# Placing the negated maxima of all groups in the query stack by small matmuls instead of by a transfer

## The chip, the cores and the metric

The kernel runs on one core of one Trainium2 chip. The metric is the device time in microseconds (us) of one execution; a kernel's time is the median of its runs. Five engines work side by side on the core: TensorE (PE), VectorE (DVE), ScalarE (ACT), GpSimd (POOL) and SyncE (SP, which only issues transfers here).

## The reference, cut to what matters

Three blocks stand one after the other: cross attention over a context of 4096 keys, a chunked retention, and a mixture of eight experts. The change lies in the first:

```python
q = split_heads(layernorm(x) @ w_q.T + b_q)        # x: (2, 256, 256), 16 heads of 16
k = split_heads(ctx @ w_k.T + b_k)                 # ctx: (2, 4096, 256)
v = split_heads(ctx @ w_v.T + b_v)
scores = einsum('bhqd,bhkd->bhqk', q, k) / 4
scores = where(mask, -inf, scores)                 # mask (1, 1, 256, 4096): True is hidden
attn = einsum('bhqk,bhkd->bhqd', softmax(scores), v)
x = x + attn @ w_o.T + b_o
x = x + retention(layernorm(x), ...)
x = x + experts(layernorm(x), ...)
```

With these inputs the mask hides all keys but the last ones, and the kernel takes a fast path over one window of 896 keys (7 blocks of 128).

## The kernel before, in words

Two batches of 16 heads are worked in eight **stages**: stage `st` is batch `st // 4` and the group of four heads `st % 4`. A stage has seven **steps**, one for each block of 128 keys (`KB = 7`), so there are 56 steps, `n = 0` to 55. Queries and keys stand cut into bf16 parts in two stacks, `qstack` and `kstack`; 96 rows of a stack carry the products of the parts, and rows 96 to 99 (`MROW` to `KROWS`) carry corrections. In `qstack` these four rows hold, for each head and query, the negated maximum of its scores, cut into bf16 parts. So one matmul yields scores less the maximum, and ScalarE needs only an exp.

The work of a step, in the order in which it is written:

- **TensorE**: scores of two heads (L847, 8 matmuls in four column groups), one or two maximum tiles of the *next* stage (L772, 8 matmuls each), scores of the two other heads, then the weighted values of the step before (L865). At the second step of a stage the output of the last stage is turned (L827).
- **ScalarE**: two exps (L1325), each over 128x512; now and then a copy of outputs (L1313), keys or values.
- **VectorE**: one reduction per maximum tile (L1647); after the eighth of a stage, four small operations cut the result into parts (L1666 to L1669, tile `mpart`).

There are two score banks, so the scores of step `n + 1` wait until the exps of step `n` have read theirs. Two pairs of banks carry the maximum tiles, so a tile waits for the reduction of the tile two before it.

**How the maxima come into the stack** differs by stage. `ROWS_AT` gives the step at which it happens: `n = 4` for stage 1, then 11, 18, 25, 32, 39 and 46 for stages 2 to 7, which is three steps ahead of the stage's own first step.

- Stage 0: before the steps begin (L808, L1471 and L1473); not touched.
- Stage 1: `second_rows`, eight transposes (L819) of 4 columns each, which land in rows 96 to 99 of the last bank, then one ScalarE copy of 4x1024 right into `qstack` (L1338).
- Stages 2 to 7: `turn_rows`, two transposes (L794) of 16 columns each, a ScalarE copy of 16x256 to `mrows` (L1297, `rows_out`), and a transfer from `mrows` to `qstack`, issued by SP (L422, `load_rows`). The first scores of the stage wait for the transfer by `rows_loaded`.

All engines run their instructions in the written order. SP issues the transfers of stages 2 to 4 between its loads of keys and late weights, and those of stages 5 to 7 behind the load of the experts' weights. A second path for other masks, which loops over windows, keeps its own way in both kernels and does not run here.

Of the kernel before, what the change touches and what calls it, by code (L numbers as in the profile page):

```python
# [16 lines left out]
P = 128  # L17
NB = 2
NQ = 256
# [10 lines left out]
G = 4  # L30
NG = NH // G
STAGES = NB * NG
# [17 lines left out]
MROW = NPROD * DK  # L50
COLS = 32
KROWS = MROW + 4
# [46 lines left out]
ROWS_AT = {LAST_TILE[st] + (2 if st > 1 else 1): st for st in range(1, STAGES)}  # L99
# [61 lines left out]
class Chunk:  # L161
# [24 lines left out]

    def rows_loaded(self, st):

        n = st // 2 + 1 - (not self.loop)
        return self.at(f"mrows_loaded{st % 2}", 16 * n) if n else self.at("mrows_ready", st + 1)  # L190

    def pair(self, kind, n):

# [10 lines left out]
def build(nc, a):  # L204
    with ExitStack() as ctx:
        def sb(name, shape, dt=F32):
            return ctx.enter_context(nc.sbuf_tensor(name, shape, dt))

        def sem(name):
            return ctx.enter_context(nc.semaphore(name))  # L210

        ident = sb("ident", [P, P])
        identb = sb("identb", [P, P], BF16)
# [58 lines left out]
        qstack = sb("qstack", [P, NH, NB, NQ], BF16)  # L272
# [9 lines left out]
        mpart = sb("mpart", [P, 2, QT, 4, G], BF16)  # L282
# [58 lines left out]
        xbank_b = bank[:, XB, :].bitcast(BF16)  # L341
# [12 lines left out]
        only = Chunk({n: sem(n) for n in [*(n for n in PER if n not in LOOP_ONLY), *("first_k_" + n for n in ("hi", "taken", "mid", "cut"))]}, 0, False)  # L354
# [23 lines left out]
        def _(sp):  # L378
# [16 lines left out]
            def stack_keys(c, n, parts=(0, 1, 2)):  # L395

                b, f = divmod(n, KIN)
                for part in parts:
                    sp.wait_ge(*c.key(("k_hi", "k_mid", "k_cut")[part], n))
                    for i in range(NPROD):  # L400
                        if K_PART[i] == part:
                            sp.dma_start(kstack[i:MROW:NPROD, b, f * HF:(f + 1) * HF, :], kpart[:, f, part, :]).then_inc(c[f"k_stacked{n}"], 16)  # L402

            def stack_edges(n, loaded):
                b, f = divmod(n, KIN)
                sp.dma_start(kstack[MROW:KROWS, b, f * HF:(f + 1) * HF, :], edge[:, :].unsqueeze(1).to_broadcast([KROWS - MROW, HF, CH])
                             ).then_inc(loaded, 16)
# [11 lines left out]
            def load_rows(c, st):  # L419
                b, g = divmod(st, NG)  # L420
                sp.wait_ge(*c.at("mrows_ready", st + 1))
                sp.dma_start(qstack[MROW:KROWS, G * g:G * g + G, b, :], mrows[:, st % 2, :]).then_inc(c[f"mrows_loaded{st % 2}"], 16)  # L422
# [36 lines left out]
            def stack_second_batch():  # L459
                for n in (2, 3):  # L460
                    stack_queries(n, (("q_hi", n), ("q_mid", n), ("q_cut", n)))

            with sp.If(fast > 0):
                stack_second_batch()
                stack_keys(only, 2)
                stack_edges(2, only["k_stacked2"])
                late_weights()
                load_rows(only, 2)
                stack_keys(only, 3)
                stack_edges(3, only["k_stacked3"])  # L470
                late_constants()
                load_rows(only, 3)
                load_rows(only, 4)
                sp.wait_ge(*only.key("k_taken", 3))
                sp.wait_ge(*only.at("v_evac", NVP + 2))
                sp.wait_ge(*only.stacked(2))
                sp.wait_ge(*only.stacked(3))
                late_experts()
                for st in range(5, STAGES):
                    load_rows(only, st)  # L480
                write_out()
            with sp.If(fast < 1):
                stack_second_batch()
# [176 lines left out]
        def _(pe):  # L660
# [120 lines left out]
            def take_last_bank(c, kind, st):  # L781

                n = XB_AT[kind, st]
                if n:
                    if c.loop:
                        settle(pe)
                    kind, st = XB_USES[n - 1]
                    pe.wait_ge(*c.at("mrows_ready" if kind == "rows" else "combined", st + 1))
# [21 lines left out]
                                           tile_position=(0, MROW), skip_group_check=True)  # L810
                    mm.then_inc(only["rows_turned"] if half_ else s["rows_begun"], 1)

            def second_rows():

                pe.wait_ge(*only.at("max_cut", 2))
                take_last_bank(only, "rows", 1)
                for j in range(G):
                    for qt in range(QT):
                        mm = pe.transpose(xbank_b[MROW:KROWS, j * NQ + qt * P:j * NQ + (qt + 1) * P], mpart[:, 1, qt, :, j], identb[:, :],  # L819
                                          tile_position=(0, MROW))  # L820
                mm.then_inc(only["rows_turned"], 1)

# [47 lines left out]
            def steps(c):  # L870
                for n in range(NU):
                    st, kt = divmod(n, KB)
                    tiles = list(TILES_AT[n])
                    if kt == 0:
                        pe.wait_ge(*c.rows_loaded(st))
                        if c.loop:
                            settle(pe)
                    scores(c, n, 0)
                    if tiles:
                        max_tile(c, tiles.pop(0))  # L880
                    if n == 0 and not c.loop:
                        pe.wait_ge(s["rows_copied"], 1)
                    scores(c, n, 1)
                    for m in tiles:
                        max_tile(c, m)
                    if n in LATER and not c.loop:
                        kind, i = LATER[n]
                        (keys if kind == "k" else later_values)(c, i)
                    if n:
                        if n == NU // NB + 1:  # L890
                            pe.wait_ge(*c.at("v_evac", NVP + 2))
                        weighted(c, n - 1)
                    if n in OUT_AT:
                        turn_outputs(c, OUT_AT[n])
                    if n in ROWS_AT and ROWS_AT[n] == 1 and not c.loop:
                        second_rows()
                    elif n in ROWS_AT:
                        turn_rows(c, ROWS_AT[n])
                    if n == AT_TURNED and not c.loop:
                        pe.wait_ge(*c.at("max_read", NT))  # L900
                        turn_at(0)
                        turn_at(1)
                    if n == AT_TURNED + 2 and not c.loop:
                        attention_out(0)
                        attention_out(1)
                if not c.loop:
                    turn_first_half()
                weighted(c, NU - 1)
                if not c.loop:
                    project_ret(0, 0)  # L910
                turn_outputs(c, STAGES - 1)
# [305 lines left out]
        def _(act):  # L1217
# [73 lines left out]
            def rows_out(c, st):  # L1291
# [4 lines left out]
                    act.wait_ge(*c.rows_loaded(st - 2))  # L1296
                act.copy(mrows[:, st % 2, :], xbank_b[0:4 * G, 0:NQ]).then_inc(c["mrows_ready"], 1)  # L1297

            def old_weight(c, st):

                act.wait_ge(*c.at("diff_ready", st + 1))
                if st >= 4:
                    settle(act)
                    act.wait_ge(*c.at("scaled", st - 3))
                act.activation(alpha[:, st % 4, :], mdiff[:, st % 2, :], ACT.Exp).then_inc(c["alpha_ready"], 1)
# [21 lines left out]
            def steps(c):  # L1327
                for n in range(NU):
                    exps(c, 2 * n)
                    exps(c, 2 * n + 1)  # L1330
                    if n in LATER and not c.loop:
                        kind, i = LATER[n]
                        (keys_out if kind == "k" else values_out)(c, i if kind == "k" else NVP + i)
                    if n and n % KB == 0:
                        outputs_out(c, n // KB - 1)
                    if n in ROWS_AT and ROWS_AT[n] == 1 and not c.loop:
                        act.wait_ge(*only.at("rows_turned", 2))
                        act.copy(qstack[MROW:KROWS, G:2 * G, 0, :], xbank_b[MROW:KROWS, :].rearrange("p (h q) -> p h q", h=G)).then_inc(only["mrows_ready"], 1)  # L1338
                    elif n in ROWS_AT:
                        rows_out(c, ROWS_AT[n])  # L1340
                        if c.loop:
                            old_weight(c, ROWS_AT[n])
                    if n == AT_TURNED + 1 and not c.loop:
                        act.wait_ge(s["wo_loaded"], 32)
                        take_at(0)
                        take_at(1)
                if not c.loop:
                    take_xn("n2", 0)
                    take_xn("n2", 1)
                outputs_out(c, STAGES - 1)  # L1350
# [589 lines left out]
```

## Time and profile before

| what | value |
|---|---|
| median of 3 runs | 229.01 us (228.62 to 231.49) |
| profiled execution: its own time | 230.21 us |
| profiled execution: its span | 228.2 us |
| PE busy | 207.8 us (91%) |
| DVE busy | 139.6 us (61%) |
| ACT busy | 110.0 us (48%) |
| POOL busy | 44.5 us (20%) |
| mean granted TensorE clock | 0.989 |

The span runs from the first to the last instruction on the core; the execution's own time holds some 2 us more around it. Attention's steps fill the time from about 40 us to 137 us of the span; retention and experts follow. Busy shares are means over parts with different limits.

### The profile page before, as it was taken

The page shows a single profiled execution, that of the slowest core. Times are in us where ns is not written, and L with a number is a line of the kernel's source. Part 1 is how long each engine was busy: PE and PEld are TensorE (multiplying, and loading weights), DVE is VectorE, ACT ScalarE, POOL GpSimd, SP SyncE. Part 2 cuts the span into 40 slices and gives each one's busy share as a digit, 9 for nine tenths or more (in the row PEclk, how much of TensorE's full clock was granted, in tenths as well). Part 3 has the DMA queues.
Part 4 walks back from the last instruction along what each step waited for, and adds up shares of the span by engine and source line. Part 5 has one row for each costly group of instructions (what it writes and reads, how often), then busy time and mean ns, then how long its engine had stood idle before and what let it go on. Part 6 is the DMA issues. An engine that isn't in the chain of part 4 may idle for free.

```text
span 228.2 us, 5747 instructions
## 1 busy us (share of the span) xinstructions
PE 207.8 (91%) x2376; PEld 125.7 (55%) x2376; DVE 139.6 (61%) x272; ACT 110.0 (48%) x238; POOL 44.5 (20%) x54
## 2 busy tenths in 40 slices
PE   8699878989899899999999997999998999999992
PEld 8358434546476575656664543545747853745340
DVE  6263738997635838988983505555346515594782
ACT  2126745758457668879788793234053061101000
POOL 8205599910072400000000100100030102010000
PEclk9799999999999999999999999999999999999998
DMA  5739965369819700280000000000000000000000
GB/s 167 247 95 240 337 167 147 90 156 207 311 47 230 201 8 6 78 293 9 4 4 4 0 3 0 0 3 1 0 0 0 3 1 0 0 23 3 27 26 27
DMA packets 15380, 18.07 MB, mean 79 GB/s; under 512 B 2596, under 2 KB 14452, under 8 KB 15348
## 3 DMA queue, kind: packets, MB, share of 16 engines
q1 hardware_dynamic: 14052, 17.29, 27.2%
q10 hardware_dynamic: 1296, 0.34, 0.8%
q8 instruction: 21, 0.34, 0.6%
q14 instruction: 11, 0.09, 0.1%
HBM read 9.79 MB, written 0.52 MB: 45 GB/s over the span
## 4 chain that ended last, share of the span: by engine, by line
PE 66%; DVE 14%; DMA 6%; ACT 5%; SPq 4%; issue 3%; POOL 1%; DVEq 0%; ACTq 0%
PE bank L1059 10%; PE bank L961 9%; DVE cneg L1647 9%; PE bank L847 8%; PE bank L865 8%; PE bank L772 7%; DMA ctxT<-in_ctxT 6%; PE bank L716 4%; PE bank L729 3%; PE bank L923 3%; PE bank L1039 3%; ACT prob L1325 3%; SPq L402 2%; PE bank L1004 2%; PE bank L943 2%
## 5 line engine op out<-in xcount | busy, mean ns | idle before, releaser
L1647 DVE TENSOR_REDUCE cneg<-bank 128x1 f32<-128x896 f32 x64 | 68.1, 1088 | 25.6 <-PE bank L772 25.3
L1325 ACT ACTIVATE prob<-bank 128x512 f32<-128x512 f32 x112 | 65.0, 599 | 15.2 <-PE bank L847 13.8
L847 PE MATMUL bank<-qstack,kstack 100*32 100x256 bf16 x896 | 46.0, 273 | 1.6 <-ACT prob L1325 0.5
L772 PE MATMUL bank<-kstack,qstack 97*32 97x448 bf16 x512 | 37.3, 353 | 3.1 <-DVE cneg L1647 3.1
L847 PEld LDWEIGHTS bank<-qstack,kstack 100*32 100x32 bf16 x896 | 22.9, 95 | 22.7 <-ACT prob L1325 9.3
L865 PE MATMUL bank<-prob,vals 128*32 128x256 f32 x448 | 35.1, 380 | 0.0
L534 POOL TENSOR_TENSOR nw<-nw,halves 128x2 f32<-128x2 f32 (+1 forms) x8 | 7.7, 966 | 127.1 <-DVE nw L1532 97.3
L961 PE MATMUL bank<-w_late,xnT 128*128 128x512 f32 x48 | 22.0, 595 | 0.0
L716 PE MATMUL bank<-ctxT,wk 128*128 128x448 f32 x32 | 14.8, 595 | 4.3 <-DMA ctxT<-in_ctxT 3.3
L772 PEld LDWEIGHTS bank<-kstack,qstack 97*32 97x32 bf16 x512 | 13.7, 96 | 9.0 <-DVE cneg L1647 4.7
L1827 DVE SCALAR_TENSOR_TENSOR x_in<-bank,nwts,x_in 128x256 f32<-128x256 f32 x32 | 15.5, 484 | 2.5 <-PE bank L1059 1.4
L1059 PE MATMUL bank<-ctxT,xnT 128*128 128x512 f32 x32 | 17.0, 613 | 0.0
L1059 PE MATMUL bank<-kpart,xnT 128*128 128x512 f32 x32 | 16.3, 592 | 0.0
L865 PEld LDWEIGHTS bank<-prob,vals 128*32 128x32 f32 x448 | 13.6, 110 | 2.6 <-issue 1.5
L729 PE MATMUL bank<-wv,ctxT 128*128 128x256 f32 x56 | 13.2, 385 | 0.1
L961 PEld LDWEIGHTS bank<-w_late,xnT 128*128 128x128 f32 x48 | 8.6, 190 | 8.1 <-issue 7.7
L729 PEld LDWEIGHTS bank<-wv,ctxT 128*128 128x128 f32 x56 | 10.3, 190 | 2.5 <-issue 1.0
L716 PEld LDWEIGHTS bank<-ctxT,wk 128*128 128x128 f32 x32 | 6.1, 203 | 9.6 <-issue 6.2
L1360 ACT ACTIVATE xnT<-bank 128x256 f32<-128x256 f32 x8 | 3.0, 384 | 15.4 <-PE bank L923 15.4
L1059 PEld LDWEIGHTS bank<-kpart,xnT 128*128 128x128 f32 x32 | 6.0, 190 | 7.3 <-issue 7.2
L1288 ACT COPY vals<-bank 128x512 f32<-128x512 f32 (+3 forms) x6 | 4.0, 659 | 8.7 <-PE bank L729 8.7
L1039 PE MATMUL bank<-w_late,kstack 128*128 128x256 f32 x32 | 7.7, 383 | 0.0
(151 smaller groups left out, 249.6 us busy)
## 6 DMA issues: line engine op xcount, KB each, us to landing
kstack<-kpart SPq DMA_DIRECT2D x24, 224.0 KB
w_late<-in_w_ret SPq DMA_DIRECT2D x1, 1536.0 KB
mask_all<-in_mask SPq DMA_DIRECT2D x2, 512.0 KB, 4.6
ctxT<-in_w_exp SPq DMA_DIRECT2D x1, 1024.0 KB
kpart<-in_w_exp SPq DMA_DIRECT2D x1, 1024.0 KB
ctxT<-in_ctxT SPq DMA_DIRECT2D x2, 448.0 KB, 6.3
ctxT<-in_ctxT SPq DMA_DIRECT2D x1, 896.0 KB, 8.9
qstack<-acc SPq DMA_DIRECT2D x12, 64.0 KB, 4.2
```

The costliest lines, as they stand in the source:

```text
L534: pool.tensor_tensor(nw[:, 3, 0:width], nw[:, 0, 0:width], halves[:, 0:width], ALU.pow).then_inc(s["root_ready"], 1)
L716: mm = pe.matmul(bank[:, c.key_banks(n) + h, 0:HC], wk[:, i, f * P:(f + 1) * P], ctxT[:, b, i, h * HC:(h + 1) * HC], start=(i == 0), stop= ...
L729: mm = pe.matmul(out[:, (k - blocks[0]) * D:(k - blocks[0] + 1) * D], ctxT[:, b, i, k * P:(k + 1) * P], wv[:, i, :], start=(i == 0), stop= ...
L772: mm = pe.matmul(out[j4:j4 + COLS, :], qstack[0:MROW + 1, h, b, qt * P + j4:qt * P + j4 + COLS], kstack[0:MROW + 1, b, h, half_ * HC:(half ...
L847: mm = pe.matmul(out[j4:j4 + COLS, hh * NQ:(hh + 1) * NQ], kstack[0:KROWS, b, h, kt * P + j4:kt * P + j4 + COLS], qstack[0:KROWS, h, b, :] ...
L865: mm = pe.matmul(bank[32 * j:32 * j + PADV, OB, 0:NQ], vals[:, b, kt, e:e + PADV], prob[:, (2 * u + j // 2) % PROBS, (j % 2) * NQ:(j % 2 + ...
L961: mm = pe.matmul(bank[:, 2 + m, :], xnT[:, c, t * P:(t + 1) * P], w_ret[:, c, m * 512:(m + 1) * 512], start=(c == 0), stop=(c == KIN - 1))
L1039: mm = pe.matmul(out[:, 0:D], yT[:, c, t * P:(t + 1) * P], w_reto[:, c, :], start=(c == 0), stop=(c == 3))
L1059: mm = pe.matmul(bank[:, PAIR_BANKS[m % 4], :], xnT[:, c, t * P:(t + 1) * P], w_exp[c][:, 2 * pr:2 * pr + 2, :], start=(c == 0), stop=(c = ...
L1325: act.activation(prob[:, n % PROBS, :], bank[:, S0 + jj, :], ACT.Exp).then_inc(c["prob_ready"], 1)
L1647: dve.tensor_reduce(cneg[:, st % 2, i:i + 1], bank[:, pair:pair + 2, 0:HC], AXXY, ALU.max, negate=True).then_inc(c["max_read"], 1)
L1827: dve.scalar_tensor_tensor(x_in[:, t, :], src, nwts[:, t, e:e + 1], x_in[:, t, :], ALU.mult, ALU.add).then_inc(s["pair_read"], 1)
```

## The change

The way of stage 1 becomes the way of stages 2 to 7 too. On TensorE `second_rows` becomes `straight_rows(st)`; on ScalarE a new function does the 4x1024 copy for any stage; SP issues no `load_rows` on this path; `rows_loaded` is then the semaphore of ScalarE's copy, `mrows_ready`.

```diff
     def rows_loaded(self, st):
-        n = st // 2 + 1 - (not self.loop)
-        return self.at(f"mrows_loaded{st % 2}", 16 * n) if n else self.at("mrows_ready", st + 1)
+        return self.at(f"mrows_loaded{st % 2}", 16 * (st // 2 + 1)) if self.loop else self.at("mrows_ready", st + 1)
...
                 late_weights()
-                load_rows(only, 2)
                 stack_keys(only, 3)
                 stack_edges(3, only["k_stacked3"])
                 late_constants()
-                load_rows(only, 3)
-                load_rows(only, 4)
...
                 late_experts()
-                for st in range(5, STAGES):
-                    load_rows(only, st)
                 write_out()
...
-            def second_rows():
-                pe.wait_ge(*only.at("max_cut", 2))
-                take_last_bank(only, "rows", 1)
+            def straight_rows(st):
+                pe.wait_ge(*only.at("max_cut", st + 1))
+                take_last_bank(only, "rows", st)
                 for j in range(G):
                     for qt in range(QT):
-                        mm = pe.transpose(xbank_b[MROW:KROWS, ...], mpart[:, 1, qt, :, j], identb[:, :],
+                        mm = pe.transpose(xbank_b[MROW:KROWS, ...], mpart[:, st % 2, qt, :, j], identb[:, :],
                                           tile_position=(0, MROW))
                 mm.then_inc(only["rows_turned"], 1)
...
+            def rows_straight_out(st):
+                b, g = divmod(st, NG)
+                act.wait_ge(*only.at("rows_turned", st + 1))
+                act.copy(qstack[MROW:KROWS, G * g:G * g + G, b, :], xbank_b[MROW:KROWS, :].rearrange("p (h q) -> p h q", h=G)
+                         ).then_inc(only["mrows_ready"], 1)
```

The callers in `steps` (L895 and L1336) now take this way for every `n` in `ROWS_AT` on the fast path.

**ScalarE, stages 3 and 4**, from the exps ahead of the rows of stage 3 on. Before:

```order
L1325 ACTIVATE prob<-bank 128x512 x8
L1288 COPY vals<-bank 128x3x16x16
L1297 COPY mrows<-bank 16x256
L1325 ACTIVATE prob<-bank 128x512 x6
L1313 COPY outT<-bank 128x256
L1325 ACTIVATE prob<-bank 128x512 x8
L1297 COPY mrows<-bank 16x256
```

After:

```order
L1325 ACTIVATE prob<-bank 128x512 x8
L1282 COPY vals<-bank 128x3x16x16
L1296 COPY qstack<-bank 4x4x256
L1325 ACTIVATE prob<-bank 128x512 x6
L1313 COPY outT<-bank 128x256
L1325 ACTIVATE prob<-bank 128x512 x8
L1296 COPY qstack<-bank 4x4x256
```

The place is the same, behind the exps of the rows' step and ahead of the six exps of the three steps before the next stage's second one; the copy itself is another.

**TensorE, the end of a rows' step** (here `n = 18`, rows of stage 3). Before:

```order
L729 MATMUL bank<-wv,ctxT 128x256 x6
L865 MATMUL bank<-prob,vals 32x256 x4
L794 MATMUL bank<-identb,mpart 16x128 x2
L847 MATMUL bank<-qstack,kstack 32x256 x8
L772 MATMUL bank<-kstack,qstack 32x448 x8
```

After:

```order
L723 MATMUL bank<-wv,ctxT 128x256 x6
L859 MATMUL bank<-prob,vals 32x256 x4
L813 MATMUL bank<-identb,mpart 4x128 x8
L841 MATMUL bank<-qstack,kstack 32x256 x8
L766 MATMUL bank<-kstack,qstack 32x448 x8
```

Eight transposes stand where two stood, ahead of the next step's scores; nothing else has moved.

**SP, from the late weights on.** Before:

```order
L426 DMA w_late<-in_w_reto 128x4x256
L422 DMA qstack<-mrows 4x4x256
L402 DMA kstack<-kpart 16x8x896 x6
L406 DMA kstack<-edge 4x8x896
L429 DMA bo_row<-in_bo 128x256
```

After:

```order
L425 DMA w_late<-in_w_reto 128x4x256
L401 DMA kstack<-kpart 16x8x896 x6
L405 DMA kstack<-edge 4x8x896
L428 DMA bo_row<-in_bo 128x256
```

The row transfer and its wait are gone; the keys' transfers follow the weights directly. The five others (two ahead of the experts' weights, three behind) are gone in the same way.

## Rows read from the trace of the kernel before

**Rows 1.** The page: busy us (share of the span) xinstructions of each engine.

```profile
PE 207.8 (91%) x2376; PEld 125.7 (55%) x2376; DVE 139.6 (61%) x272; ACT 110.0 (48%) x238; POOL 44.5 (20%) x54
```

**Rows 2.** The page: chain of waits, share of the span by line.

```profile
PE bank L1059 10%; PE bank L961 9%; DVE cneg L1647 9%; PE bank L847 8%; PE bank L865 8%; PE bank L772 7%; DMA ctxT<-in_ctxT 6%; PE bank L716 4%; PE bank L729 3%; PE bank L923 3%; PE bank L1039 3%; ACT prob L1325 3%; SPq L402 2%; PE bank L1004 2%; PE bank L943 2%
```

**Rows 3.** The chain in order of time, steps 25 to 30: start us, us, what.

```profile
91.50 0.56 PE bank L772 x8
...
98.60 0.41 PE bank L772 x8
...
99.03 1.10 DVE cneg L1647
```

**Rows 4.** Timeline of ScalarE around step 25: start, us, engine, line, out<-in, [idle before].

```profile
92.33 0.60 ACT L1325 ACTIVATE prob<-bank 128x512 f32<-128x512 f32 x1 [0.56 <-PE bank L847]
92.85 0.36 ACT L1297 COPY mrows<-bank 16x256 bf16<-16x256 bf16 x1
93.12 3.74 ACT L1325 ACTIVATE prob<-bank 128x512 f32<-128x512 f32 x6
96.75 0.37 ACT L1313 COPY outT<-bank 128x256 f32<-128x256 f32 x1
```

**Rows 5.** Timeline of TensorE, steps 25 to 29.

```profile
92.11 0.61 PE L865 MATMUL bank<-prob,vals 128*32 128x256 f32 x8
...
92.54 0.22 PE L794 MATMUL bank<-identb,mpart 128*16 128x128 bf16 x1
...
93.80 0.39 PE L847 MATMUL bank<-qstack,kstack 100*32 100x256 bf16 x7
...
97.29 0.60 PE L865 MATMUL bank<-prob,vals 128*32 128x256 f32 x8
...
97.83 0.44 PE L827 MATMUL bank<-ident,outT 128*128 128x128 f32 x2
```

**Rows 6.** Timeline of TensorE's weight loads, first scores of stage 4.

```profile
95.20 0.12 PEld L847 LDWEIGHTS bank<-qstack,kstack 100*32 100x32 bf16 x8 [0.35 <-DMA qstack<-mrows]
```

**Rows 7.** Waits of the whole trace: who waited for whom, us, times, longest us.

```profile
PEld bank L847 <- DMA qstack<-mrows: 1.5, 4, 0.4
```

**Rows 8.** Timeline of TensorE and ScalarE, steps 4 to 6, with stage 1's rows.

```profile
49.12 0.60 PE L865 MATMUL bank<-prob,vals 128*32 128x256 f32 x8
...
49.56 0.44 PE L819 MATMUL bank<-identb,mpart 128*4 128x128 bf16 x5
...
50.21 1.00 ACT L1338 COPY qstack<-bank 4x1024 bf16<-4x1024 bf16 x1 [0.27 <-PE bank L819]
...
51.24 1.08 ACT L1325 ACTIVATE prob<-bank 128x512 f32<-128x512 f32 x2
...
51.89 0.40 PE L847 MATMUL bank<-qstack,kstack 100*32 100x256 bf16 x8 [0.46 <-ACT prob L1325]
...
53.15 0.39 PE L847 MATMUL bank<-qstack,kstack 100*32 100x256 bf16 x8
```

**Rows 9.** Timeline of TensorE, step 12, value projection.

```profile
65.79 3.72 PE L729 MATMUL bank<-wv,ctxT 128*128 128x256 f32 x16
```

**Rows 10.** Timeline of TensorE and its weight loads, steps 20 and 21.

```profile
83.36 0.49 PE L847 MATMUL bank<-qstack,kstack 100*32 100x256 bf16 x8
...
84.84 0.12 PEld L847 LDWEIGHTS bank<-qstack,kstack 100*32 100x32 bf16 x8 [0.43 <-DMA qstack<-mrows]
```

**Rows 11.** Timeline of ScalarE, steps 46 and 47.

```profile
122.75 0.36 ACT L1297 COPY mrows<-bank 16x256 bf16<-16x256 bf16 x1
123.69 1.08 ACT L1325 ACTIVATE prob<-bank 128x512 f32<-128x512 f32 x2 [0.57 <-PE bank L847]
```

**Rows 12.** Busy time by windows: stretch, length, engines, PEclk, DMA share, GB/s.

```profile
50.80:52.00 1.20, 0.74 (x14) 0.26 (x10) 1.09 (x1) 1.18 (x3) 0.00 (x0) 1.00 1.08 242
...
91.50:101.90 10.40, 10.02 (x240) 6.55 (x244) 9.29 (x14) 8.65 (x17) 0.00 (x0) 1.00 0.62 201
101.90:112.20 10.30, 9.96 (x236) 6.50 (x236) 9.18 (x14) 8.54 (x17) 0.00 (x0) 1.00 0.03 7
```

More of the change, by code:

```diff
@@ L811, in first_rows @@
                     mm.then_inc(only["rows_turned"] if half_ else s["rows_begun"], 1)
-            def second_rows():
-                pe.wait_ge(*only.at("max_cut", 2))
-                take_last_bank(only, "rows", 1)
+            def straight_rows(st):
+                pe.wait_ge(*only.at("max_cut", st + 1))
+                take_last_bank(only, "rows", st)
                 for j in range(G):
                     for qt in range(QT):
-                        mm = pe.transpose(xbank_b[MROW:KROWS, j * NQ + qt * P:j * NQ + (qt + 1) * P], mpart[:, 1, qt, :, j], identb[:, :],
+                        mm = pe.transpose(xbank_b[MROW:KROWS, j * NQ + qt * P:j * NQ + (qt + 1) * P], mpart[:, st % 2, qt, :, j], identb[:, :],
                                           tile_position=(0, MROW))
@@ L894, in steps @@
                         turn_outputs(c, OUT_AT[n])
-                    if n in ROWS_AT and ROWS_AT[n] == 1 and not c.loop:
-                        second_rows()
+                    if n in ROWS_AT and not c.loop:
+                        straight_rows(ROWS_AT[n])
                     elif n in ROWS_AT:
@@ L1335, in steps @@
                         outputs_out(c, n // KB - 1)
-                    if n in ROWS_AT and ROWS_AT[n] == 1 and not c.loop:
-                        act.wait_ge(*only.at("rows_turned", 2))
-                        act.copy(qstack[MROW:KROWS, G:2 * G, 0, :], xbank_b[MROW:KROWS, :].rearrange("p (h q) -> p h q", h=G)).then_inc(only["mrows_ready"], 1)
+                    if n in ROWS_AT and not c.loop:
+                        rows_straight_out(ROWS_AT[n])
                     elif n in ROWS_AT:
```

## The prediction, made before the changed kernel had run

> **What bounds the kernel now.** The page's first part comes first: TensorE is busy 91% of the span, ScalarE 48%, VectorE 61% [rows 1]. Those are means over very unlike parts, so they only say where to look. The chain by line [rows 2] names TensorE's scores, maximum tiles and weighted values (L847, L772, L865), together 23% of the span, the maximum reductions (L1647, 9%), and ScalarE's exps with 3%. The transfer of the rows is not in it. This speaks for asking what the change puts on TensorE and ScalarE, not what it takes from SP.
>
> Next, the chain in order of time [rows 3]. Within a stage it runs on TensorE from the tile at 91.50 (step 25, in which the rows of stage 4 are turned) to the tile at 98.60, crosses to VectorE at 99.03 for the last reduction of the group and those behind it, and comes back at the same place one stage later. So the rows' step stands right at the start of TensorE's part of the loop. What delays a score there delays the tile at 98.60, hence VectorE, hence the next stage: nothing further on waits for anything else.
>
> Then, how much slack ScalarE has just there. It waits 0.56 us for the scores at 92.33, *ahead* of the rows' copy, and none behind it: after the copy at 92.85 six exps follow without a gap, 3.74 us in all, and at 96.75 the output copy right behind them [rows 4]. That is (3.74 - 0.60) / 5 = 0.63 us per exp, 1.26 us per step. TensorE takes the same time: the transposes of step 25 start at 92.54, the scores of step 27 at 93.80 [rows 5], 1.26 later. The exp those scores need ends at 93.12 + 0.60 = 93.72. Its slack is 0.08 us. Both engines are bounds here, each with nothing to spare.
>
> **The change part by part.**
>
> *Removed: six transfers.* The first scores of a stage wait for them four times, 1.5 us together on the weight loads, at most 0.4 each [rows 7]. On the matmuls it is less: the scores of stage 4 could follow those of 93.80 by one step of 1.26, at 95.06; they start at 95.20 [rows 5, 6]. That wait costs 0.14. For stage 3 it is 84.84 - 83.36 - 1.26 = 0.22 [rows 10]; stages 5 and 6 repeat stage 4. Stages 2 and 7 do not wait. All that this part can give is 0.22 + 3 x 0.14 = 0.64 us. SP's own queue costs nothing: the issues behind the removed waits (keys of the last half batch, experts' weights) are needed many steps later, and the experts' 2 MB, which come earlier now, disturb nobody: stage 4, with a DMA share of 0.62, took 10.40 us, stage 5, with 0.03, took 10.30 [rows 12].
>
> *Added: a longer copy and six more transposes, at each of six steps.* Here the trace has the price itself, since stage 1 already goes this way [rows 8]. The transposes start at 49.56, the copy at 50.21 and takes 1.00 (the old one 0.36), the next exp starts at 51.24, and the scores behind it at 51.89, after TensorE has stood idle 0.46. From first transpose to those scores: 2.33 us. The same stretch of stage 4 takes 93.80 - 92.54 = 1.26 [rows 5]. **The rows' step gets 1.07 us longer.** Of this, 0.34 is that the copy starts 0.65 instead of 0.31 behind the first transpose, and the rest is the copy.
>
> *What of it stays.* After that step both engines run at 1.26 again (51.89 to 53.15 [rows 8]), so nothing is caught up inside the stage, except that the wait for the transfer falls away. VectorE only gets more slack. The output copy still fits: it would end near 98.2, where the weighted values, moved from 97.29 [rows 5] to 98.2, ask for its bank; a margin of nothing, and I add nothing.
>
> Stage by stage:
>
> - Stage 2 (`n = 11`): step 12 holds the value projection, 3.72 us of TensorE from 65.79 on [rows 9], for which no exp is needed. The copy hides behind it; only the transposes stay. Five started at 49.56 take 0.44 [rows 8], one takes 0.22 [rows 5], so each adds 0.055, and six more 0.33.
> - Stage 3 (`n = 18`): 1.07 - 0.22 = 0.85. The projection of this step lies ahead of the rows and covers nothing.
> - Stages 4, 5, 6: 1.07 - 0.14 = 0.93 each, 2.79.
> - Stage 7 (`n = 46`): ScalarE has 0.57 of slack behind the copy [rows 11]. The copy starts 0.34 later, at 123.09; the next exp can start at 123.09 + 1.03 = 124.12 instead of 123.69: 0.43.
>
> Sum: 0.33 + 0.85 + 2.79 + 0.43 = **4.4 us more.** Against its own execution this is a span of 228.2 + 4.4 = 232.6 and a time of 230.2 + 4.4 = 234.6. That execution was 1.2 over the median of the runs, so the time is forecast from the median: 229.0 + 4.4 = **233.4 us**. Bounds of the four full steps: 1.07 each if the return of the transfer's wait does not come, 0.64 each (1.00 - 0.36, the copies alone) if the later start of the copy is covered. That makes 3.3 to 5.0 for the forecast's own case, 232.3 to 234.0.
>
> *A switch of array layout.* The old transposes use the array at full width, between matmuls in column groups; the new ones stay in a column group. In the trace the weighted values and the transposes start 0.43 apart before (92.11 to 92.54 [rows 5]) and 0.44 apart on the new way (49.12 to 49.56 [rows 8]): no switch is seen to cost anything, and the sum has no term for it. The Trainium skill (TensorEngine Tiling (Array Packing), Tiling Modes) says otherwise: changing the tiling mode drains the engine. By it the change would save two switches at each step; this is the fourth rival below.
>
> *The clock.* TensorE gets six more idle stretches. In the one that stage 1 has already, between 50.80 and 52.00, the granted clock was 1.00 [rows 12]. No term.
>
> **The rivals.**
>
> 1. *Slower still: nothing is given back and the slack beyond is gone.* Each of the six steps costs 1.07, stage 2's and stage 7's too: 6.4, 235.4 us. It would take a second wait: the output copy, pushed behind the exps, arrives late at the weighted values, or the maximum tiles slip into a new wait for VectorE. For it: the margin of nothing above. Against: the projection of stage 2 is three times as long as the copy. 20%.
> 2. *Not slower: the copy disappears in ScalarE's idle time.* ScalarE is busy 8.65 of 10.40 us in stage 4 [rows 12]; 1.75 are free. If the exps behind the copy could use them, only the transfers' waits would change: 229.0 - 0.6 = 228.4 us. The point from which this decides is a slack of 1.07 behind the copy; the rows show 0.08, the free time lies ahead of it (0.56 at 92.33 [rows 4]). With a part of it used, anything between 228.4 and 232.3. 9%.
> 3. *The change does not do what it says*, and a transfer or a wait stays: the order of the instructions excludes this, no chance.
> 4. *The switch of layout was being paid*, hidden in a place the starts do not show. Its nearest price is the turning of the outputs, also at full width: the transposes start 97.83 - 97.29 = 0.54 behind the weighted values instead of 0.43 [rows 5], so 0.1 per switch, two per step, six steps: 1.3 saved, 229.0 + 4.4 - 1.3 = 232.1 us. 4%.
> 5. *TensorE's clock falls in the new gaps*: no row shows it; a percent or more on top, above 235. 3%.
>
> **How the numbers follow.** The forecast has 64%, the rivals 20, 9, 0, 4 and 3%. Median noise widens each by some 0.5. Two per cent of 229.0, about what a measurement of this kernel can tell from no change, ends at 233.6, hard above my number. Of the forecast's 64%, some 24 lie above it and 40 below; with rivals 1 and 5 this makes 45% for slower by over 2%. Within 2%: 40, most of rival 2 and all of rival 4, 53%. Faster by over 2%: 2%; nothing in the trace offers 4.6 us. The range goes from 231.8, under rival 4, to 235.4, rival 1's value; it leaves out most of rival 2, the upper half of rival 1 and rival 5, and the forecast's tails, near 2 in 10.
>
> **What would show it.** In the changed kernel's trace: seven ScalarE copies of 4x1024 near 1.00 us; from the first of the eight transposes to the second next scores 2.3 us in steps 18, 25, 32 and 39, with 0.4 to 0.5 of TensorE idle, waiting for ScalarE; step 12 unchanged but for 0.3; stages 4 to 6 of 11.3 us instead of 10.4 (distance of the first tiles behind VectorE's group end); no wait for a transfer of rows. I would be wrong if the later exps close up faster than 0.63 us each, if the scores in the rows' step did not wait for the copy, or if the retention and the experts took another time than before, since nothing of them is touched.

## The result: 233.25 us, 1.9% slower

| | before | changed |
|---|---|---|
| median, 4 runs each | 229.12 us (228.62 to 231.49) | 233.25 us (232.32 to 233.46) |
| ratio, 95% interval | | 1.0194 (1.0146 to 1.0242) |
| profiled execution: span | 228.2 us | 230.3 us |
| ACT busy | 110.0 us | 114.2 us |

The forecast was 233.4 us (231.8 to 235.4). The changed kernel was run once more later (experiment 7), and that run took 235.28 us, near the forecast's upper end. The ratio's interval straddles the 2% line, on which the forecast had put nearly even chances. Here and below, medians are of all runs and ratios of those in which the granted clock was undisturbed, so a ratio can differ from that of the medians.

### The profile page after: what moved, and what is told of

The parts are those of the page before. It is cut to its first block, busy times and chain, and to the rows that moved or that the text cites. A ratio compares the mean times of both kernels' runs of the same rounds, so it can differ in the third digit from the quotient of the medians.

```text
span 230.3 us, 5807 instructions
## 1 busy us (share of the span) xinstructions
PE 209.3 (91%) x2412; PEld 127.0 (55%) x2412; DVE 139.7 (61%) x272; ACT 114.2 (50%) x238; POOL 44.4 (19%) x54
## 2 busy tenths in 40 slices
DMA packets 15260, 18.02 MB, mean 78 GB/s; under 512 B 2572, under 2 KB 14332, under 8 KB 15228
## 4 chain that ended last, share of the span: by engine, by line
PE 64%; DVE 12%; DMA 6%; ACT 6%; issue 5%; SPq 4%; POOL 1%; ACTq 0%; DVEq 0%
PE bank L1053 10%; PE bank L955 9%; PE bank L841 8%; DVE cneg L1646 8%; PE bank L859 7%; PE bank L766 6%; DMA ctxT<-in_ctxT 6%; ACT prob L1325 4%; PE bank L710 4%; PE bank L723 3%; PE bank L1033 3%; PE bank L917 3%; SPq L401 2%; PE bank L998 2%; PE bank L937 2%
## 5 line engine op out<-in xcount | busy, mean ns | idle before, releaser
L841 PE MATMUL bank<-qstack,kstack 100*32 100x256 bf16 x896 | 46.7, 274 | 4.3 <-ACT prob L1325 2.3
L841 PEld LDWEIGHTS bank<-qstack,kstack 100*32 100x32 bf16 x896 | 22.7, 95 | 26.5 <-ACT prob L1325 12.4
L710 PE MATMUL bank<-ctxT,wk 128*128 128x448 f32 x32 | 13.4, 551 | 3.5 <-DMA ctxT<-in_ctxT 2.5
L1296 ACT COPY qstack<-bank 4x1024 bf16<-4x1024 bf16 x7 | 7.0, 1004 | 1.8 <-PE bank L813 1.8
```

The lines of the kernel that those rows point to most:

```text
L710: mm = pe.matmul(bank[:, c.key_banks(n) + h, 0:HC], wk[:, i, f * P:(f + 1) * P], ctxT[:, b, i, h * HC:(h + 1) * HC], start=(i == 0), stop= ...
L841: mm = pe.matmul(out[j4:j4 + COLS, hh * NQ:(hh + 1) * NQ], kstack[0:KROWS, b, h, kt * P + j4:kt * P + j4 + COLS], qstack[0:KROWS, h, b, :] ...
L1296: act.copy(qstack[MROW:KROWS, G * g:G * g + G, b, :], xbank_b[MROW:KROWS, :].rearrange("p (h q) -> p h q", h=G)).then_inc(only["mrows_read ...
```

## The profile after

The page's first part and its chain, of the changed kernel, in the form of [rows 1] and [rows 2]:

```profile
PE 209.3 (91%) x2412; PEld 127.0 (55%) x2412; DVE 139.7 (61%) x272; ACT 114.2 (50%) x238; POOL 44.4 (19%) x54
PE bank L1053 10%; PE bank L955 9%; PE bank L841 8%; DVE cneg L1646 8%; PE bank L859 7%; PE bank L766 6%; DMA ctxT<-in_ctxT 6%; ACT prob L1325 4%; PE bank L710 4%; PE bank L723 3%; PE bank L1033 3%; PE bank L917 3%; SPq L401 2%; PE bank L998 2%; PE bank L937 2%
```

TensorE has 36 more matmuls, ScalarE the same number of instructions, 4.2 us more of them; ScalarE's exps rise to 4% of the chain. The page lists the new copy as one group (line, engine, out<-in, count | busy, mean ns | idle before):

```profile
L1296 ACT COPY qstack<-bank 4x1024 bf16<-4x1024 bf16 x7 | 7.0, 1004 | 1.8 <-PE bank L813 1.8
```

The rows' step of stage 4, TensorE's timeline and then ScalarE's, against [rows 4] and [rows 5]:

```profile
91.49 0.44 PE L813 MATMUL bank<-identb,mpart 128*4 128x128 bf16 x5
...
93.81 0.40 PE L841 MATMUL bank<-qstack,kstack 100*32 100x256 bf16 x8 [0.46 <-ACT prob L1325]
...
95.08 0.39 PE L841 MATMUL bank<-qstack,kstack 100*32 100x256 bf16 x8
```

```profile
92.13 1.00 ACT L1296 COPY qstack<-bank 4x1024 bf16<-4x1024 bf16 x1 [0.28 <-PE bank L813]
93.16 3.56 ACT L1325 ACTIVATE prob<-bank 128x512 f32<-128x512 f32 x6
```

From the first transpose to the scores behind the copy it is 93.81 - 91.49 = 2.32 us, where it was 1.26. TensorE stands idle 0.46 us for ScalarE, as it did in stage 1 before [rows 8]. The next step is 1.27, and no first scores of a stage wait for a transfer.

**Where the time went, stage by stage.** The two spans cannot be compared directly: the profiled execution before lost time at its start (last section). So I measure between instructions that both kernels have: the turnings of the outputs (L827 before, L821 after) at steps 8, 15, 22, 29, 36, 43, 50 and behind the last step. Each interval holds the rows' step of one stage. TensorE's timeline of the changed kernel has them as in these two rows; the one at step 29 stood at 97.83 before [rows 5]:

```profile
97.69 0.44 PE L821 MATMUL bank<-ident,outT 128*128 128x128 f32 x2
...
108.98 0.44 PE L821 MATMUL bank<-ident,outT 128*128 128x128 f32 x2
```

All eight starts, before: 55.76, 73.82, 87.46, 97.83, 108.20, 118.56, 129.94, 138.99; changed: 53.05, 71.42, 85.92, 97.69, 108.98, 120.27, 132.09, 141.14. Their distances in us, with those of every experiment's profile, one execution each:

| kernel | stage 2 | 3 | 4 | 5 | 6 | 7 | rest | sum |
|---|---|---|---|---|---|---|---|---|
| before | 18.06 | 13.64 | 10.37 | 10.37 | 10.36 | 11.38 | 9.05 | 83.23 |
| changed | 18.37 | 14.50 | 11.77 | 11.29 | 11.29 | 11.82 | 9.05 | 88.09 |
| four_copies | 18.01 | 14.43 | 11.15 | 11.22 | 11.15 | 11.48 | 9.05 | 86.49 |
| more_turns | 18.26 | 13.86 | 10.62 | 11.15 | 10.60 | 11.61 | 9.05 | 85.15 |
| two_copies | 18.40 | 15.42 | 12.95 | 12.20 | 12.21 | 12.73 | 9.05 | 92.96 |
| early_transfer | 18.02 | 13.40 | 10.20 | 10.31 | 10.21 | 11.71 | 9.05 | 82.90 |
| early_straight | 18.81 | 13.41 | 12.22 | 10.56 | 10.54 | 12.11 | 9.05 | 86.70 |
| late_experts | 18.39 | 14.50 | 11.30 | 12.20 | 11.28 | 11.82 | 9.06 | 88.55 |
| before_early_experts | 18.00 | 13.64 | 11.30 | 10.34 | 10.36 | 11.38 | 9.06 | 84.08 |
| experts_last | 18.37 | 14.50 | 11.30 | 11.30 | 11.30 | 11.82 | 9.05 | 87.64 |
| after_again | 18.36 | 14.51 | 12.32 | 11.29 | 11.30 | 11.82 | 9.05 | 88.65 |
| best_transfer | 18.02 | 13.41 | 10.20 | 10.21 | 10.21 | 11.38 | 9.05 | 82.48 |

Undisturbed stages repeat within some 0.03 us between executions, so differences of a tenth can be read here, far below what the medians tell. The changed kernel takes 4.86 us more: 0.31, 0.86, 1.40, 0.92, 0.93, 0.44 and 0. Behind the last turning both take the same, 228.2 - 138.99 = 89.2 and 230.3 - 141.14 = 89.2.

**One thing the forecast does not hold.** Stage 4 costs 1.40 instead of 0.93. TensorE stops in the midst of a score group of step 24:

```profile
88.16 0.28 PE L841 MATMUL bank<-qstack,kstack 100*32 100x256 bf16 x3
89.21 0.38 PE L841 MATMUL bank<-qstack,kstack 100*32 100x256 bf16 x5 [0.77 <-issue]
```

Three matmuls of eight run, then 0.77 us of "issue", a wait with no named cause. The windows around it (length, busy time of the engines, PEclk, DMA share, GB/s) show what ends just there, the loads of the experts:

```profile
84.00:88.00 4.00, 4.00 (x102) 2.50 (x96) 3.28 (x4) 3.40 (x8) 0.00 (x0) 1.00 1.02 339
88.00:90.00 2.00, 1.23 (x31) 0.87 (x27) 1.80 (x6) 0.97 (x2) 0.00 (x0) 1.00 0.05 15
```

SP issued them at 80.24, where it had been 94.07 before: the waits that stood ahead of the removed transfers no longer hold SP back.

## The experiments

**1. four_copies: ScalarE's part alone, in the old way.** (`spare` is unused room.)

```diff
             def rows_out(c, st):
+                if not c.loop:
+                    for i in range(3):
+                        act.copy(spare[0:4 * G, i, :], xbank_b[0:4 * G, 0:NQ])
                 act.copy(mrows[:, st % 2, :], xbank_b[0:4 * G, 0:NQ]).then_inc(c["mrows_ready"], 1)
```

> The old way with its two transposes and its transfer, but ScalarE copies the 16x256 tile three times more, into spare room, before the copy that counts: 0.36 + 3 x 0.27 = 1.17 us in place of 0.36, +0.81, and nothing more on TensorE. Theory (a longer copy on ScalarE, between exps that have no slack, is the cost): +0.81 in stages 3, 4, 5 and 6, since the transfer too is issued 0.81 later and its wait is not given back; stage 2 hides it behind the value projection; stage 7 has 0.57 of slack, +0.24. Sum 3.5 us, 232.6. Rival (the six transposes are the cost, ScalarE has room): no change, 229.1. Rival (part of the copy goes into idle time): between.

Measured: +3.26 us over the stages. Stages 3 to 6 cost 0.79, 0.78, 0.85 and 0.79, stage 2 nothing, stage 7 0.10 (expected 0.24). At step 25 ScalarE's three extra copies put the one that counts off by 92.13 - 91.34 = 0.79 us. Medians 231.32 against 228.17, ratio 1.0178 (1.008 to 1.0276). Time on ScalarE at this place is paid one for one in stages 3 to 6, and the projection covers it in stage 2. The rival that ScalarE has room there is refuted.

**2. more_turns: TensorE's part alone.**

```diff
             def turn_rows(c, st):
                 take_last_bank(c, "rows", st)
+                if not c.loop:
+                    for j in range(1, G):
+                        for qt in range(QT):
+                            pe.transpose(xbank_b[MROW:KROWS, j * NQ + ...], mpart[:, st % 2, qt, :, j], identb[:, :],
+                                         tile_position=(0, MROW))
```

> The old way with its one copy of 16x256 and its transfer, and six transposes of 4 columns more ahead of the two old ones, which no copy reads. Theory (both engines are bounds, so the later start of the copy counts): the copy starts 0.33 later, all behind it too: 0.33 in each of stages 2 to 7 less 0.08 of slack in four of them, 1.7 us, 230.8. Rival (the transposes run beside the scores in other column groups and cost nothing; all of the loss is the copy): 229.1. Rival (a switch of layout between the two kinds of transposes is dear): over 2.5 us.

Measured: 0.20 to 0.25 in every stage, 0.78 in stage 5, where a pause fell again (0.70 us of "issue" at 101.47). Sum 1.92, without the pause some 1.4. So the transposes are not free. In stages 3, 4 and 6 the cost is the 0.25 that was expected; in stages 2 and 7 it is less than the 0.33. At step 39 (stage 6) the copy starts 0.77 us behind the start of the exp before it, where it was 0.52, so here too the stage pays what the copy is late. On a switch of layout this run says nothing: the step still enters and leaves the full width once, as before. Its medians, 233.29 against 228.17, ratio 1.0188 (1.0076 to 1.03), say more than its stages do. In the profiled execution 1.7 us more went behind the last turning (90.9), where the granted clock was 0.91 for 20 us. The mean granted clock of its four runs was 0.976 to 0.987, that of the runs before behind the ratio 0.990 to 1.000. This fits the rest, but why the clock was lower is not known.

**3. two_copies: double the suspected cost.**

```diff
             def rows_straight_out(st):
...
                 act.wait_ge(*only.at("rows_turned", st + 1))
+                if st > 1:
+                    act.copy(spare[MROW:KROWS, :, :], xbank_b[MROW:KROWS, :].rearrange("p (h q) -> p h q", h=G))
```

> The changed kernel, with each 4x1024 copy of stages 2 to 7 done twice, the first time into spare room: +1.0 us on ScalarE per stage. Theory: 1.0 more in stages 3 to 7 (in stage 7 the slack is used up by the first copy), none in stage 2, where 2.36 us of ScalarE's wait for the value projection are left: 5 us on top of the changed kernel, 238.3. Rival (the delay saturates, since VectorE or the maximum tiles become the bound and catch part of it up): under 3 us more.

Measured: 237.86 us, ratio to before 1.0443 (1.0366 to 1.052). Over the changed kernel 4.87 us: 0.03 in stage 2, then 0.92, 1.18, 0.91, 0.92 and 0.91. The second copy starts 0.91 behind the first (105.54 and 106.45 in stage 5), so each stage again pays what ScalarE is later. The 1.18 of stage 4 holds a longer pause: 1.04 us of "issue" at 90.41, where the changed kernel has 0.77. TensorE's wait for the exps between 55 and 142 us, in the changed kernel and in this one (who waited for whom, us, times, longest):

```profile
PE bank L841 <- ACT prob L1325: 1.8, 4, 0.5
```

```profile
PE bank L842 <- ACT prob L1328: 6.5, 5, 1.4
```

4 waits of 0.46 become 5, four of them 0.9 longer and one new. Nothing saturates; no other engine became the bound.

**4. early_transfer: the old way, at another place in the step.**

```diff
                     scores(c, n, 0)
+                    if n in ROWS_AT and ROWS_AT[n] > 1 and not c.loop:
+                        turn_rows(c, ROWS_AT[n])
                     if tiles:
...
                     exps(c, 2 * n)
+                    if n in ROWS_AT and ROWS_AT[n] > 1 and not c.loop:
+                        rows_out(c, ROWS_AT[n])
                     exps(c, 2 * n + 1)
```

(The calls at the step's end go.)

> The old way (two transposes, 16x256 copy, transfer), but written earlier inside the same step: the transposes behind the first scores, where TensorE then waits 0.37 us for VectorE, and the copy between the two exps, where ScalarE waits 0.56 us. Theory (the place in the step decides what a copy costs): copy and transposes become free, the transfer is issued 1.1 us earlier and its wait of 0.14 to 0.22 goes too; 0.2 to 0.4 per stage in stages 3 to 6, 228.1. Rival (the place does not matter, only the engines' sums): no change but for the transfer's wait, 0.6 at most. Rival (the copy delays the second exp): slower.

ScalarE's timeline, step 25:

```profile
89.76 0.60 ACT L1327 ACTIVATE prob<-bank 128x512 f32<-128x512 f32 x1 [0.44 <-PE bank L847]
90.25 0.34 ACT L1299 COPY mrows<-bank 16x256 bf16<-16x256 bf16 x1
90.91 4.36 ACT L1327 ACTIVATE prob<-bank 128x512 f32<-128x512 f32 x7 [0.32 <-PE bank L847]
```

The copy lies in the idle time, as meant, and 0.32 us of that are left. Measured: 0.24, 0.17, 0.06 and 0.15 less in stages 3 to 6, under my 0.2 to 0.4 for most (stage 5 holds a pause of 0.39 us of "issue"). Together that is 0.62, and the rival, that only the transfer's wait goes, had said 0.6 at most. So this run does not decide for the place in the step: the rows' step took 1.26 us already, like its neighbours, and a copy of 0.36 cost nothing where it stood. Experiment 5 decides. Stage 7 lost 0.33; its transposes come before the parts are cut:

```profile
120.31 0.22 PE L794 MATMUL bank<-identb,mpart 128*16 128x128 bf16 x1 [0.42 <-DVE mpart L1673]
```

Sum -0.33; medians 229.02 against 228.17 with a ratio of 1.0005 (0.9958 to 1.0052): no change that can be measured. The forecast of 228.1 was a miss in size.

**5. early_straight: the changed kernel with both calls moved the same way** (same edit, with `straight_rows` and `rows_straight_out`).

> The changed kernel, with the transposes of stages 2 to 7 written behind the first scores of the same step and the 4x1024 copy between its two exps, where ScalarE waits 0.56 us for scores. Theory (only the part of the copy that outlasts the idle time counts): transposes hidden in TensorE's wait for VectorE; stages 4 to 6 +0.3 each for the second exp, less the transfer's wait 0.14; stage 3 hidden behind the value projection; stage 7 +0.4; with the pause of TensorE near the experts' loads 1.1 us over the kernel before from the copy of stage 1 to the end of the span (179.1), time 229.6 to 230.3. Rival (the copy costs its 1.0 us wherever it stands): 182 and more, as the changed kernel.

Measured: 0.19 and 0.18 over the kernel before in stages 5 and 6, where the place at the step's end costs 0.92 and 0.93; stage 3 is 0.23 *shorter*. So in these two stages four fifths of the loss hung on the place. Two terms were missed: stage 2 costs 0.75 (there is no idle time between its exps, and the second scores of step 12 stand behind the exp that the copy pushes, TensorE idle for 0.26), stage 7 0.73 (as in experiment 4, its transposes wait for the parts to be cut). In stage 4 TensorE paused for 1.44 us of "issue". The sum is +3.47, of which the pause is a large part; medians 233.26 against 229.41, ratio 1.0209 (1.0135 to 1.0283), well over the 229.6 to 230.3 I expected.

**6. late_experts and before_early_experts: only the loads moved.**

```diff
                 sp.wait_ge(*only.stacked(3))
+                sp.wait_ge(*only.at("mrows_ready", 5))
                 late_experts()
```

> The changed kernel, with the experts' 2 MB held on SP until the rows of stage 4 are placed, as in the kernel before, where they stood behind that stage's transfer. Nothing else differs. In the changed kernel these loads ran some 13 us earlier, and TensorE stood still for 0.77 us in the midst of a score group at step 24, waiting for nothing the profile shows, just as the loads ended. Theory (the fetch of TensorE's instructions queues behind the loads): the pause leaves step 24; either it is gone, 0.5 us less from the copy of stage 1 to the end of the span (182.3 instead of 182.8), or it turns up beside the loads' new place. Rival (the pause belongs to the code's position): it stays at step 24 with 0.77 us.

```diff
                 load_rows(only, 3)
-                load_rows(only, 4)
                 sp.wait_ge(*only.key("k_taken", 3))
...
                 late_experts()
-                for st in range(5, STAGES):
+                for st in range(4, STAGES):
                     load_rows(only, st)
```

> The kernel before, with the experts' 2 MB issued ahead of the rows of stage 4 instead of behind them, so that they run near step 20 to 24, as in the changed kernel. Theory (removing the transfers' waits moved the loads, and that alone brings the pause): a pause of TensorE of 0.5 to 1 us near step 22 to 25, and the rows' transfer of stage 4 may land later, up to some us, behind the 2 MB. Rival (the loads' place is harmless; the pause hangs on where TensorE's program stands, which has 36 more transposes in the changed kernel): 178.0 us from the copy of stage 1 to the end of the span, as before.

The pauses, from TensorE's timeline of the first, then of the second:

```profile
100.06 0.55 PE L767 MATMUL bank<-kstack,qstack 97*32 97x448 bf16 x7
101.71 0.36 PE L767 MATMUL bank<-kstack,qstack 97*32 97x448 bf16 x1 [1.10 <-issue]
```

```profile
90.50 0.55 PE L771 MATMUL bank<-kstack,qstack 97*32 97x448 bf16 x7
92.21 0.35 PE L771 MATMUL bank<-kstack,qstack 97*32 97x448 bf16 x1 [1.17 <-issue]
```

With the loads issued at 93.17, the changed kernel has a clean stage 4 (11.30) and a spoilt stage 5 (12.20). With the loads issued at 84.30, the kernel before gets a pause too, and stage 4 goes from 10.37 to 11.30 with not one instruction of TensorE changed. So where the loads stand brings the pause about. late_experts: 234.36 against 229.41 us, ratio 1.0245 (1.0173 to 1.0317); before_early_experts: one run, 231.93.

**7. experts_last and after_again.** The first issues the loads behind the last stage, on a semaphore of their own (the waits for the late weights then count two loads fewer):

```diff
+                sp.wait_ge(*only.at("outT_ready", STAGES))
                 late_experts()
...
+                pe.wait_ge(s["experts_loaded"], 32)
                 pair(0, 0)
```

> The changed kernel, with the experts' 2 MB issued only after the last stage, on a semaphore of their own, some 45 us ahead of their use. From the turning of the first stage's outputs to that of the last the changed kernel took 88.09 us, with one pause of 0.77 us. Theory (the pause is a fetch of instructions behind the loads): no pause of TensorE without a named cause in the eight stages, since nothing large is loaded there any more; stage 4 back from 11.77 to 11.29, 87.6 us in all, time 232.8. Where it goes: none or little behind the last stage, where TensorE runs few instructions per us. Rival (some other cause, of which the loads only shift the time): a pause of 0.5 us or more stays within the stages, 88.1 or more.

> The changed kernel once more, for the size and place of the pause. Theory: the same stages to 0.02 us, but for stage 4, where the pause stands at the same instruction of step 24 with a length that may differ by some tenths (0.77 before), since the loads set it and not the program alone.

experts_last has no pause in the stages and stages 4 to 6 alike at 11.30; 87.64 in all, as expected, and 89.2 behind the last turning, so nothing came back there. Median 232.76, ratio 1.0163 (1.01 to 1.0227). after_again shows the changed kernel's own pause at the very same cut, three matmuls and five:

```profile
91.78 0.38 PE L841 MATMUL bank<-qstack,kstack 100*32 100x256 bf16 x5 [1.32 <-issue]
```

It lasts 1.32 us instead of 0.77, all other stages within 0.01. This run took 235.28 us: against the first profile its start was 2.03 us longer, stage 4 0.55 and the part behind the last turning 0.36. So the pause needs both: a fixed place of TensorE's program, and loads that run shortly before TensorE gets there.

**8. best_transfer: what the experiments point to.** early_transfer for stages 2 to 6 only, with the experts' loads as in experts_last.

> The old way with transposes and copy written early in the step, for stages 2 to 6 only (in stage 7 the early place cost 0.33 us, since the transposes then wait for VectorE), and the experts' loads behind the last stage. Theory (place decides): 0.66 less than the kernel before from the first to the last turning of outputs, 82.6 against 83.2 us, time 228.4, at most just visible. Rival (the old place was as good): 83.2.

Measured: 82.48 us over the stages, 0.75 less than before, 5.61 less than the changed kernel; stage 7 is back at 11.38. Median of 12 runs 228.77 against 229.38 of 16, ratio 1.0 (0.9957 to 1.0044). It beats the changed kernel; over the kernel before the stages show a gain of 0.3%, which the times cannot show.

## Why the prediction was right, point by point

- **What bounds.** "Both engines are bounds here, each with nothing to spare": holds. Extra ScalarE time is paid one for one (experiments 1 and 3), extra transposes by as much as they make the copy late (2). The slack was smaller than the 0.08 us read off: where TensorE waits for an exp, its scores start 0.05 behind the exp's end (93.16 + 0.60 = 93.76, then 93.81), so some 0.03 was left.
- **The rows' step gets 1.07 us longer**, read off stage 1: measured 2.32 - 1.26 = 1.06, with the same 0.46 of idle TensorE.
- **What the transfers give back**, 0.14 per stage and 0.22 in stage 3: holds, as the net costs of 0.92, 0.93 and 0.86 against 0.93, 0.93 and 0.85 show.
- **Stage 2**, hidden but for the transposes: 0.31 for 0.33. **Stage 7**: 0.44 for 0.43.
- **SP's queue costs nothing**: this step failed, the only one that did. "The experts' 2 MB, which come earlier now, disturb nobody" was read from stage 4 before, which had the loads and no pause. But the pause comes at fixed places of TensorE's program, and in the kernel before, the packet that the last section takes for TensorE's next instructions was late too, but still in time by less than 0.3 us. It costs 0.47 us here and 1.03 in after_again.
- **The sum**: 4.4 forecast, 4.86 in the stages, 4.39 without the pause. The medians moved by 4.1, and a start of the program that varies by more than this difference lies between them. So that the median fell within 0.2 us of the forecast is in part luck.
- **Rival 1** (something gives way beyond the copy) did not come; even doubled copies cost what they last. **Rival 2** failed at the point named for it: the idle time is ahead of the copy. With the copy moved there (5) most of it does vanish, in stages 5 and 6.
- **Rival 4**, the switch of layout, of which the Trainium skill (TensorEngine Tiling (Array Packing), Tiling Modes) says that it drains the engine: weighted values and transposes start 0.44 apart after, in a column group, as they did 0.43 apart at full width [rows 5]; so no cost can be seen here either, and no experiment took a switch away on its own:

```profile
102.34 0.61 PE L859 MATMUL bank<-prob,vals 128*32 128x256 f32 x8
102.78 0.44 PE L813 MATMUL bank<-identb,mpart 128*4 128x128 bf16 x5
```

- **Rival 5**: the granted clock was 1.00 in all stage windows read.

## What to carry to other kernels

A transfer that is waited for by 0.14 us is worth 0.14 us; the copy that replaces it is worth its whole length if it stands in a train of instructions without a gap. Look for the gap first: the same copy half a step earlier cost 0.2 instead of 0.9 in two stages, but 0.7 in two others (no gap in one, parts not yet cut in the other). When waits are taken out of a queue, ask what else moves with it, since a bulk load that starts earlier can delay what was just in time before.

## What was not expected of the hardware

**Bulk loads can stop TensorE at fixed places of its program.** Seven profiles show one pause of 0.70 to 1.44 us each (an eighth, early_transfer, one of 0.39) while or just after 2 MB are loaded at some 300 GB/s, and the changed kernel's two profiles have it at the same matmul. Without such loads in the stages (experts_last, best_transfer) there is none. The page counts the fetch of instructions as a queue of its own; its row (packets, MB, share of 16 engines), changed kernel:

```profile
q8 instruction: 21, 0.34, 0.7%
```

The single packets and TensorE's records in the traces tie the pause to this queue:

- The 21 packets, 16 KB each, follow TensorE's progress: one comes for some 240 of its 4956 recorded instructions (weight loads, matmuls, its sequencer's). So I take them for blocks of its program.
- Counted in TensorE's instructions, the eight pauses stand at two places only. Five are at TensorE's 1098th recorded matmul, in kernels where this is a score (L841, L842) and in before_early_experts, where it is a maximum tile (L771). Three are at the 1351st or 1352nd (more_turns, early_transfer, late_experts).
- Each pause ends 2.44 to 2.66 us behind the start of one packet; in the changed kernel it is 89.21 - 86.55. That packet started 5 to 8 us after the loads were issued. TensorE had by then got as far as its record 2165 to 2197; in the profiles without the loads there it was at 2000 to 2078 when the same packet started. For the second place it was 2659 to 2695 against 2516 to 2568.
- The kernel before and four_copies had this packet just as late (99.19 and 98.54, records 2650 and 2654). TensorE came to its 1352nd matmul 2.68 and 2.67 us behind it, and there was no pause.

All this fits one reading: the loads hold up a block of TensorE's instructions, and the pause is what is left of that delay when TensorE gets to the block. It rests on the times in twelve profiles; no experiment moved the fetch itself.

**The start of the program varies.** The first turning of outputs stands at 55.76 before and at 53.05, 55.08 and 56.34 in three profiles of kernels that do the same up to there. In the execution before, TensorE idled 1.92 us for the first context, and the windows (before, then changed) show the granted clock behind it:

```profile
7.00:11.00 4.00, 3.27 (x8) 1.84 (x9) 0.73 (x2) 0.47 (x1) 0.41 (x1) 0.67 0.74 254
```

```profile
7.00:11.00 4.00, 3.15 (x12) 1.83 (x13) 1.30 (x3) 1.11 (x2) 0.41 (x1) 1.00 0.79 270
```

Part of that stretch ran at 1.2 instead of 2.4 GHz: the first four projections took 2.70 us instead of 1.74. These 0.96 us and 0.8 more of waiting for the context are most of the 2.71 us by which the first turning came later before; the rest was not traced. So two spans that differ by 2.1 us hide a difference of 4.86 in the stages.
